# Local attention over four pairs of heads: one written-out program in place of a first pass, a loop and a rest, on TensorE, VectorE and ScalarE

## The reference, cut to what matters

```python
def local_attention(q, k, v):
    b, h, n, d = q.shape
    w = n // WINDOW                                    # WINDOW = 128
    bq = q.reshape(b, h, w, WINDOW, d) * QK_SCALE
    ...
    bk, bv = (look_around(bk), look_around(bv))        # window w-1 beside window w
    sim = jnp.einsum('bhwid,bhwjd->bhwij', bq, bk)
    mask = (i < j) | (i > j + WINDOW) | (j == -1)
    sim = jnp.where(mask, -jnp.finfo(sim.dtype).max, sim)
    attn = jax.nn.softmax(sim, axis=-1)
    out = jnp.einsum('bhwij,bhwjd->bhwid', attn, bv)
    return out.reshape(b, h, n, d)
...
x = L0_attn_x
x = _layernorm(x + _L0_attn_ref(...)); x = _layernorm(x + _L0_ffn_ref(...))   # 2 local layers
... # relative-bias attention, block-scaled projection, state scan, experts, recurrence
x = _layernorm(x + _L3_ffn_ref(...))                                          # 2 local layers
```

## Time and profile before

| | |
|---|---|
| median of 3 runs | 7962.52 us (7954.46 to 7972.7) |
| the profiled execution, its own time | 7959.56 us |
| its span, first to last instruction | 7957.9 us |
| PE busy over the span | 6620.0 us (83%) |
| DVE busy | 4763.3 us (60%) |
| ACT busy | 2802.6 us (35%) |
| POOL busy | 1320.0 us (17%) |
| instructions fetched: packets on queue 14, on queue 8 | 287, 105 |

### The profile page before, as it was taken

One profiled execution on the slowest core, in us unless ns is written; L12 is line 12 of the kernel. 1 busy time (PEld: TensorE's weight loads), 2 busy tenths in 40 slices (PEclk: granted clock), 3 DMA queues, 4 the chain that ended last, 5 costly groups with the idle time before them and its releaser, 6 DMA issues. The chain is left out here.

```text
span 7957.9 us, 122287 instructions
## 1 busy us (share of the span) xinstructions
PE 6620.0 (83%) x30596; PEld 3410.1 (43%) x30596; DVE 4763.3 (60%) x12029; ACT 2802.6 (35%) x6066; POOL 1320.0 (17%) x779
## 2 busy tenths in 40 slices
PE   6799958989987966989988357996997788898979
PEld 2333334655455533222222244333554445544555
DVE  5655547733763634877775764996334675347635
ACT  0255524712462200555554111552110256124611
POOL 1110106100610003000000000551001441006100
PEclk9899989999998987999999678998998899999989
DMA  5322244542455256222221322113322345324541
GB/s 176 106 60 58 56 118 147 185 141 60 146 173 171 77 204 192 67 68 63 60 68 48 107 84 75 37 36 115 75 64 70 118 154 169 123 78 151 174 144 55
DMA packets 930584, 850.14 MB, mean 107 GB/s; under 512 B 240136, under 2 KB 786912, under 8 KB 929952
## 3 DMA queue, kind: packets, MB, share of 16 engines
q1 hardware_dynamic: 500624, 522.99, 23.0%
q10 hardware_dynamic: 429568, 323.08, 13.1%
HBM read 503.10 MB, written 346.00 MB: 107 GB/s over the span
## 5 line engine op out<-in xcount | busy, mean ns | idle before, releaser
L1243 ACT ACTIVATE Catt_E<-Catt_t 128x512 f32<-128x512 f32 x1024 | 577.6, 596 | 505.3 <-DVE Catt_t L1206 307.9
L1180 DVE CUSTOM_DVE_ANT_0 Catt_S<-Catt_s,Catt_win 128x1024 f32<-128x1024 f32 x512 | 620.8, 1214 | 5.9 <-DMA Catt_win<-skewed 3.7
L1180 DVE CUSTOM_DVE_ANT_0 Aatt_S<-Aatt_s,Aatt_win 128x128 f32<-128x128 f32 (+7 forms) x512 | 377.1, 756 | 303.8 <-PE Aatt_s L1110 297.7
L1160 PE MATMUL Catt_o<-Catt_E,Catt_V 128*32 128x256 f32 (+1 forms) x3840 | 549.5, 405 | 0.0
L1243 ACT ACTIVATE Aatt_E<-Aatt_t 128x512 f32<-128x512 f32 (+3 forms) x768 | 354.7, 489 | 326.8 <-PE Aatt_t L1142 251.5
L1206 DVE TENSOR_TENSOR Catt_t<-Catt_t,Catt_near 128x256 f32<-128x256 f32 (+2 forms) x640 | 281.7, 456 | 268.1 <-PE Catt_t L1139 234.6
L1139 PE MATMUL Catt_t<-Catt_Q,Catt_K 123*128 123x512 bf16 x1024 | 328.8, 389 | 92.8 <-ACT Catt_E L1243 73.4
L1110 PE MATMUL Catt_s<-Catt_K,Catt_Q 96*128 96x512 bf16 x1024 | 325.3, 401 | 23.4 <-DMA Catt_K<-k_parts 12.3
L1160 PE MATMUL Aatt_o<-Aatt_E,Aatt_V 128*32 128x256 f32 (+2 forms) x2304 | 323.8, 388 | 0.0
L1160 PEld LDWEIGHTS Catt_o<-Catt_E,Catt_V 128*32 128x32 f32 x3840 | 180.5, 110 | 272.9 <-issue 185.6
L2336 PE MATMUL scan_cum<-scan_X,scan_upto 128*128 128x512 f32 x512 | 265.8, 609 | 25.1 <-DVE scan_X L2405 23.7
(11 more groups left out here) (721 smaller groups left out, 14605.8 us busy)
## 6 DMA issues: line engine op xcount, KB each, us to landing
moe_cb<-c_s SPq DMA_DIRECT2D x16, 1024.0 KB, 10.5
bias_rows<-line SPq DMA_DIRECT2D x16, 960.0 KB, 6.3
skewed<-bias_win ACTq DMA_DIRECT2D x16, 960.0 KB
Catt_win<-skewed SPq DMA_DIRECT2D x16, 960.0 KB, 4.7
rec<-state_in_r ACTq DMA_DIRECT2D x32, 416.0 KB
scan_r<-rec SPq DMA_DIRECT2D x64, 208.0 KB, 2.5
Aatt_Q<-q_parts SPq DMA_DIRECT2D x32, 384.0 KB, 4.3
Aatt_K<-k_parts SPq DMA_DIRECT2D x32, 384.0 KB, 5.6
```

Source lines behind the costliest of these rows:

```text
L1160: ins = t.matmul(o_ps[f:f + 2 * hd, x:y], V[:, b, kb, h, :], E[:, kb % NB, h, x:y], start=kb == 0, stop=kb == end and y == hi)
L1180: v.tensor_tensor_reduce(out=S[:, j % 2, 0:w], in0=s_ps[j % 2][:, 0:w], in1=win[:, 0 if causal else h, w0:w0 + w], scale=-1.0, scalar=BIG, ...
L1243: a.activation(E[:, kb % NB, h, lo:hi], t_ps[n % 2][:, 0:hi - lo], ACT.Exp, scale=scale).then_inc(exped, 1)
```

## The change

A second helper, `written_out`, takes the same list and emits count x steps steps with plain Python numbers for pass and step. TensorE, VectorE and ScalarE of local attention use it; SyncE keeps `pipelined`, GpSimd its loop. The functions called are the same, with constants in place of the loop's register. `pipelined` itself and all its other uses stay.

```diff
--- before.py
+++ after.py
@@ -96,6 +96,14 @@
             run(it, i)
     for i in range(steps, steps + max(lag for lag, _ in parts)):
         run(count - 1, i)
+
+
+def written_out(eng, count, steps, parts):
+
+    for i in range(count * steps + max(lag for lag, _ in parts)):
+        for lag, fn in parts:
+            if 0 <= i - lag < count * steps:
+                fn((i - lag) // steps, (i - lag) % steps)
 
 
 def rows_of(act, b, t0, n):
@@ -775,7 +783,7 @@
-            pipelined(t, PAIRS, ST, ((0, scores), (5, values), (3, turn), (3, turn_sums)))
+            written_out(t, PAIRS, ST, ((0, scores), (5, values), (3, turn), (3, turn_sums)))
@@ -816,7 +824,7 @@
-            pipelined(v, PAIRS, ST, ((0, mask), (1, invert), (3, move), (3, move_sums)))
+            written_out(v, PAIRS, ST, ((0, mask), (1, invert), (3, move), (3, move_sums)))
@@ -849,7 +857,7 @@
-            pipelined(a, PAIRS, ST, ((0, exp), (3, move), (6, move_o)))
+            written_out(a, PAIRS, ST, ((0, exp), (3, move), (6, move_o)))
```

## The result

| | before | after |
|---|---|---|
| median | 7962.52 us (7954.46 to 7972.7, 5 runs) | 7922.92 us (7915.31 to 7930.28, 5 runs) |
| after / before | | 0.9951 (0.9937 to 0.9966) |
| profiled execution, its span | 7959.56, 7957.9 | 7922.92, 7921.2 |

The forecast was 7926.0. The two profiled executions are 7959.56 - 7922.92 = 36.6 us apart, where the sum said 36.5. That the two agree to 0.1 us is luck, since single stages that were not changed differ by up to 4.3 us between the two.

What follows compares the result with a forecast made beforehand. TensorE's full queue was taken to bound local attention's steady state. Removing 36.18 us at the seams and 0.3 us of branch cost, with zero for fetches and moved code, made 36.5 us: 7962.5 to 7926.0 us, range 7908 to 7944.

Steps and rivals of the forecast that it cites:

- The bound: Local attention's passes: TensorE's queue is full and sets 13.92 us for eight steps; register instructions cost nothing that shows.
- The seams: Between passes of B1att, H0att and H1att: waits at six loop branches go, 12.13, 10.37 and 13.68 us, 36.18 in all.
- the fourth rival: Local attention's seams: VectorE waits for something tied to the pass, not code, so the wait stays: 7962 us; 4 in 100.
- The branch without a wait: Local attention's loops: branch and register instructions cost 0.1 us a stage where nothing waits, 0.3 to 0.4 in all.
- Fetches in new code: Passes 1 to 3 of local attention, now written out: fetching their code costs nothing; upper bound 65 us.
- the first rival: Written-out passes of local attention: one fetch too late in each of 12 adds 65 us, 7991 us; 5 in 100.
- Moved code: All code behind B0att shifts, so other loops lie elsewhere; value taken zero.
- The second rival: B1ffn, H1ffn and experts loops no longer fit once moved: 30 us lost, 7956, one loop 7932 to 7938; 9 in 100.
- The third rival: Relative-bias attention (Catt) comes to lie better and loses its six waits, 32.8 us: 7893 us; 4 in 100.
- Catt should wait wherever it lies: Relative-bias attention: its body, longer than local attention's, keeps its branch waits after the move, 33 us.

## Why the prediction was right

- **The bound.** TensorE's full queue sets the rate inside a pass, 13.92 us for eight steps, with or without register instructions. It holds: 165.74 us in each stage after, and 165.74 with TensorE and ScalarE back in their loops.
- **The seams, 36.18 us.** Right in place, kind and size. The stages gave 12.12, 10.37 and 13.68 us. That it is code and not something tied to the pass, the fourth rival, was argued then and is shown by the moved loops and by the packets, five a pass or none.
- **The branch without a wait, 0.3 us.** Too small to tell, and the part of the sum that no run shows. B0att gave nothing from pass 1 on: pass 1 was 55.87 us and is 55.67, but what follows is longer by as much.
- **Fetches in new code, nothing.** Right; the first rival (7991) is out. Four or five packets a pass on queue 8, where three or four were forecast, and three to six on queue 14 are hidden.
- **Moved code, nothing.** Right in the sum. The second rival can happen: the same moves, made on purpose, gave the gated network and the experts waits that they didn't have, 4.3 and 4.2 us. And one loop was hit by the change itself, TensorE's in Catt, 2.4 to 2.8 us at each of six branches. I had weighed VectorE's loops only; that it cost nothing is luck, as it was hidden by VectorE's own waits. The third rival didn't happen: Catt's body, with 465 instructions, more than three stretches of 128 hold (384), waited at its six branches in each of the nine kernels that keep it.
- **"Catt should wait wherever it lies"**, 33 us: 33.9.

The median is 3 us under the forecast, within the runs' scatter.

## What to carry to other kernels

Look at each engine's first instruction behind a loop's backward branch: a wait of some 5 us with "issue" beside it, in one copy of a stage and not in another, was code that is fetched again here, and it took the other engines down with it and TensorE's clock too, to 0.50 for 6.5 us. The word alone doesn't prove it: in the kernel before ScalarE has a wait of 2.08 us on "issue" at 1027.43 us that stands behind two transfers which it issues itself (1.89 us), with no packet on queue 14. Count the packets of the instruction queues in a pass of the loop. Write out the one engine that waits, or move its loop by a few instructions; in local attention the others' loops cost nothing (165.74 us either way). When one engine's wait is gone look for the next one's, which may have hidden behind it, and after any change in the length of a program look at the loops behind it.

## What the runs showed of the hardware that was not expected

- The loop body of 350 instructions stayed with VectorE where it touched three stretches of 128 instructions, and was fetched again where it touched four: the eleven starts tried from 4 to 36 had no wait and no packet on queue 14, the nine from 40 to 127 had a wait and five packets a pass. Two stretches of 256, the size that a packet of queue 8 would give (16 KB at 64 bytes), don't fit the runs: with them a body of 350 has 163 free starts in a row; counted modulo 256 the bodies of B0att, B1att, H0att and H1att start at 64, 182, 157 and 19, and any 163 in a row that hold 64 hold 19 or 157 too, so that H1att or H0att would have been free, and both wait (6.39 and 5.13 us).
- The wait at a missed branch of VectorE is not one number: 4.75 to 7.91 us in local attention, 4.3 in the gated network and 4.2 in the experts, and TensorE's is 2.4 to 2.9. VectorE goes on 2.1 to 3.0 us after the start of the last packet on queue 14 ahead of it, in all these stages; the difference lies before that packet, which starts 1.7 to 1.8 us into the wait in the gated network and the experts and 2.6 to 5.6 us into it in local attention. The DMA engines are busy for 0.31 and 0.02 of the wait in the former two and for 0.43 to 0.88 in local attention, but inside local attention the busier waits are not the longer ones (5.86 us at 0.88, 7.91 at 0.58). Why the packet comes late is open.
